# A five-stage graph network on one core: in message layers two to five the addition of edge features and the relu take an octet of row tiles by one instruction each

## The reference, cut to what matters

```
for l in range(5):
    h_in = h + vn[batch]
    emsg = relu(h_in[src] + edge_attr @ We[l] + be[l])
    agg  = segment_sum(emsg, dst, num_segments=4096)
    t = h_in + agg
    t = relu(t @ W1[l] + b1[l]) @ W2[l] + b2[l]
    ...                      # normalisation, relu but in the last layer
    h = t + h_in
```

## Time and profile before

| what | value |
| --- | --- |
| median of 3 runs | 9367.71 us (9363.5 to 9368.68) |
| profiled execution | 9374.53 us |
| its span, first to last instruction | 9372.7 us |
| mean granted TensorE clock | 0.786 of full speed |
| TensorE matmuls busy | 6152.2 us, 66% |
| VectorE busy | 3611.3 us, 39% |
| ScalarE busy | 1609.9 us, 17% |
| GpSimd busy | 5231.5 us, 56% |

### The profile page before, as it was taken

How to read it: one execution, slowest core, us unless ns; L and a number is a source line. 1 busy time by engine, 2 the same in 40 slices (tenths; PEclk the granted TensorE clock), 3 DMA queues, 4 the chain that set the end, 5 groups by cost and what they waited for, 6 DMA issues and landing times. The chain is left out here.

```text
span 9372.7 us, 114718 instructions
## 1 busy us (share of the span) xinstructions
PE 6152.2 (66%) x28483; PEld 4699.3 (50%) x28484; DVE 3611.3 (39%) x5667; ACT 1609.9 (17%) x3223; POOL 5231.5 (56%) x5128
## 2 busy tenths in 40 slices
PE   3667667765776667556856783656666666666666
PEld 2556545654565456445644562444453453454345
DVE  4445434443443334334543453545561121122123
ACT  1222212221222112212200013332330000000000
POOL 3555465546554655555557744543316676766666
PEclk8889878887888788778877886777786776777677
DMA  4333333333333333333333315554423332332333
GB/s 121 105 100 99 99 106 97 96 96 104 102 93 97 105 101 96 98 105 100 105 92 87 89 58 190 197 177 158 144 86 92 95 93 87 93 94 83 90 95 89
DMA packets 434518, 987.02 MB, mean 105 GB/s; under 512 B 124176, under 2 KB 210832, under 8 KB 417936
## 3 DMA queue, kind: packets, MB, share of 16 engines
q0 software_dynamic: 245760, 673.51, 25.1%
q1 hardware_dynamic: 128816, 194.88, 6.3%
q10 hardware_dynamic: 59744, 116.68, 3.8%
HBM read 845.23 MB, written 139.46 MB: 105 GB/s over the span
## 5 line engine op out<-in xcount | busy, mean ns | idle before, releaser
L371 POOL DMA_INDIRECT ring<-node_table,idx x4608 | 4711.4, 1022 | 3306.6 <-issue 2091.2
L382 PE MATMUL psE<-ring,shared 128*128 128x256 f32 x3072 | 1027.7, 471 | 449.0 <-issue 338.3
L987 DVE TENSOR_TENSOR ring<-ring,psE 128x1024 f32<-128x1024 f32 x640 | 762.5, 1218 | 1048.8 <-issue 436.1
L382 PEld LDWEIGHTS psE<-ring,shared 128*128 128x128 f32 x3072 | 660.7, 229 | 791.6 <-issue 502.0
L263 DVE SCALAR_TENSOR_TENSOR shared<-iota,block_start,dst_f 128x1024 f32<-128x1024 f32 x352 | 450.8, 1286 | 1395.0 <-remote 817.4
L1364 POOL DMA_INDIRECT ring<-att_table,idx x512 | 519.2, 1014 | 764.8 <-ACT idx L1568 496.1
L851 ACT ACTIVATE ring<-ring 128x1024 f32<-128x1024 f32 x640 | 661.9, 1060 | 937.2 <-DVE ring L987 673.8
L397 PE MATMUL psE<-ring,stk 128*128 128x256 f32 x1984 | 545.5, 429 | 248.8 <-DVE stk L263 133.6
L691 PE MATMUL psE<-we_stk,stk 128*128 128x256 bf16 x2560 | 394.5, 296 | 451.1 <-issue 161.8
L382 PE MATMUL psAT<-ring,shared 128*128 128x256 f32 x2560 | 653.1, 410 | 47.9 <-issue 47.9
L382 PE MATMUL psAT<-ring,S 128*128 128x256 f32 x2560 | 649.6, 409 | 30.1 <-issue 30.0
(11 more groups left out here) (356 smaller groups left out, 7018.0 us busy)
## 6 DMA issues: line engine op xcount, KB each, us to landing
ring<-node_table,idx POOLq DMA_INDIRECT x4608
rows_table<-ring SPq DMA_DIRECT2D x64, 1072.0 KB
ring<-rows_table ACTq DMA_DIRECT2D x64, 1072.0 KB
stk<-stack_table SPq DMA_DIRECT2D x128, 512.0 KB
node_table<-tab ACTq DMA_DIRECT2D x251, 128.0 KB
stack_table<-stk SPq DMA_DIRECT2D x64, 256.0 KB
ring<-att_table,idx POOLq DMA_INDIRECT x512
tab<-in_x ACTq DMA_DIRECT2D x35, 128.0 KB
```

Of the source, the lines that this page charges most:

```text
L371: nc.gpsimd.indirect_dma_start(ring[:, q, 0:gw], None, table, bass.IndirectOffsetOnAxis(ap=idx[:, RING * half + q:RING * half + q + 1], ax ...
L382: ins = nc.tensor.matmul(bank, hots[:, u, :], ring[:, U * ob + u, 0:D], start=False, stop=True, skip_group_check=True)
L987: nc.vector.tensor_tensor(ring[:, q:q + 4, 0:D], ring[:, q:q + 4, 0:D], psE[:, 4 * D * g:4 * D * g + 4 * D].rearrange("p (u f) -> p u f", ...
```

## The change

In message layers two to five (l > 0) one addition and one relu take all eight row tiles of an octet. The addition waits for eight gathers and both halves of the encode, and signals `added[0]` alone; the relu waits for that and signals `message[0]` alone. The encode of the next octet waits for `added[0]` before its first half and for nothing before its second; the first unit waits for `message[0]` at tile 0 alone. The first message layer is as before.

```diff
@@ encode, TensorE
                         for g in halves:
-                            if not first:
+                            if not first and (l == 0 or g == 0):
                                 pe.wait_ge(added[g], at_pe)
@@ ready, TensorE, before the matmuls of the first unit
-                                if u % 4 == 0:
+                                if u % (4 if l == 0 else U) == 0:
                                     pe.wait_ge(message[u // 4], at_pe)
@@ ScalarE
-                            for g in halves:
+                            for g in halves if l == 0 else (0,):
                                 q = U * ob + 4 * g
+                                tiles = 4 if l == 0 else U
                                 act.wait_ge(added[g], at_act)
-                                nc.scalar.activation(ring[:, q:q + 4, 0:D], ring[:, q:q + 4, 0:D], ACT.Relu
+                                nc.scalar.activation(ring[:, q:q + tiles, 0:D], ring[:, q:q + tiles, 0:D], ACT.Relu
                                                      ).then_inc(message[g], 1)
@@ VectorE
-                            for g in halves:
+                            for g in halves if l == 0 else (0,):
                                 q = U * ob + 4 * g
-                                for t in range(q, q + 4):
+                                tiles = 4 if l == 0 else U
+                                for t in range(q, q + tiles):
                                     dve.wait_ge(gathered[t], landed)
 
                                 dve.wait_ge(encoded[g], at_dve)
-                                nc.vector.tensor_tensor(ring[:, q:q + 4, 0:D], ring[:, q:q + 4, 0:D],
-                                                        psE[:, 4 * D * g:4 * D * g + 4 * D].rearrange(
-                                                            "p (u f) -> p u f", u=4), ALU.add).then_inc(added[g], 1)
+                                if l > 0:
+                                    dve.wait_ge(encoded[1], at_dve)
+                                nc.vector.tensor_tensor(ring[:, q:q + tiles, 0:D], ring[:, q:q + tiles, 0:D],
+                                                        psE[:, D * 4 * g:D * (4 * g + tiles)].rearrange(
+                                                            "p (u f) -> p u f", u=tiles), ALU.add).then_inc(added[g], 1)
```

## The result

The changed kernel took 9400.98 us (median of 6 runs, 9375.85 to 9418.46) against 9365.60 us for the kernel before in the same comparison (6 runs, 9346.53 to 9379.42): ratio 1.0036, interval 1.0019 to 1.0053, that is 35 us and 18 to 50 by the interval. Two later comparisons of the same pair, on two chips, gave 1.0012 (0.9998 to 1.0025) and 1.0020 (1.0006 to 1.0034). The three, weighted by their intervals, give 1.0021, some 20 us slower.

What follows compares the result with a forecast made beforehand. No engine is near full; what counts is which engine is late, and that changes within a layer. Losses of 1.2, 4.2 and 1.8 us a layer gave 29 us, 9397 on the median, plus 3: 9400; range 9352 to 9455.

Steps and rivals of the forecast that it cites:

- (a): Layer start: the next encode starts behind the whole addition, 1.07 us later, plus some 0.1 for waits; 1.2 us a layer.
- (b): Last 11 to 12 octets of a layer: first unit waits for the whole relu, 0.35 us an octet, 4.2 a layer.
- TensorE is paced by its own chain: End of a layer: hidden-layer matmuls, their relu, turn, encode, first and further unit set TensorE's pace; no size given.
- R2: End of a layer: further unit or hidden relu absorbs the first unit's delay; 0 to 18 us remain, 9377; chance 0.19.
- (c): Middle, about octets 5 to 51: delays between a gather burst's start and the silence's end are swallowed; 1.8 us a layer kept.
- (d): Stack loads, VectorE's next one-hot, GpSimd's queue: loads 1 us later cost nothing, and GpSimd gets no new instruction.
- R1: Message layers: silences move, every delay is kept, 22 us a layer, 90 in all, 9458; chance 0.12 including anything towards the forecast.
- silences: Middle of a layer: VectorE and TensorE nearly idle from late instructions, recovering about 3 us after a gather burst's last.
- Code loading: Middle of a layer: a taken branch forces a DMA instruction fetch, tying a silence to that moment; no size given.
- R3: Starved stretch: ScalarE's missing relu gives back 0.7 us a turn, 45 us less the 29: 16 us faster, 9352; chance 0.12.

Runs made afterwards that it cites:

- late_halves: Kernel before with its two additions and two relus, but everything that follows waits until both halves are done: 9372.21 us, ratio 1.0019.
- one_add: Changed kernel with its one wide addition, but the relu in two halves with two signals: 9370.07 us, ratio 1.0017.
- one_relu: Kernel before with two additions, but one wide relu behind both: 9342.22 us, ratio 0.9991; repeated, 9362.77 us, ratio 1.0002.
- before_pad: Kernel before with one more ScalarE register instruction (adding 0) per octet in layers two to five: 9360.92 us, ratio 1.0000.
- relu_twice: Changed kernel with its wide relu carried out twice in layers two to five: 9438.17 us, ratio 1.0086 to the kernel before.

## Why the prediction was right, and where it was not

The forecast was 9400, 32 us over the median, on a sum of 29; measured were 35 us in the first comparison and some 20 over the three, both within the 14 to 48 of its bounds. The sign and the size held, but the size by luck as well: 24 of the 29 us stood on terms of which the runs show 4 or 5. By terms:

**(a) The encode and gathers at the layer's start.** Predicted 1.2 us a layer; the gathers resume 1.3 us a layer later, 5.4 in four, of which 4.3 are the later signal and 1.1 the longer wait in front of the addition. Right. late_halves and one_add have it too (gathers 6.1 and 5.4 us later than before in four layers), one_relu has not, and of these only the two that have it are slower than the kernel before by more than their interval.

**(b) The first unit behind the relu.** Its first half held: 0.35 us an octet were taken and the first unit starts 1.45 instead of 1.08 us after the encode, 0.37 more. Its second half failed. "TensorE is paced by its own chain" is the step that was wrong. Paid by all of 12 octets the delay would be 4.2 us a layer; 1.0 a layer is what three profiles of each show for octets 52 to 63 (4.2 in all, one pair of them +11.5, the others +0.2 and +1.0). The octets without a hidden relu, and the last, do pay it in full, 4.9 us in four layers. In the octets from 55 to 60 TensorE waits before the turn for a hidden relu that stands at encode + 12.8 us whether the matmuls before it ended 4.65, 3.90 or 3.34 us earlier. The first unit's delay comes out of that wait of TensorE, 2.4 us in the median before and 1.6 with the change, and costs nothing; with the relu done twice the wait is used up in half of these octets, and they pay 23 us. This is rival R2's mechanism. What I held against it, "that idle time is caused by a relu that itself waits for matmuls behind the first unit, so it moves along", was read from the order of the program and not from the trace, whose lines on L712 and L805 above have the matmuls done 4.66 us before the relu. Its "remote" as the relu's releaser said as much. Why the relu stands there is open: it needs the gathers beside it (0.04 us behind the matmuls without them), and ScalarE's own DMA issue before it is a cause that no run excludes.

**(c) The middle swallows.** Right, and stronger than taken: 1.8 us a layer were predicted, -0.4 measured, which is nothing within the scatter. Without gathers the same octets pay 38 us, and octets 0 to 12 another 29; with them, nothing that shows.

**(d) Nothing elsewhere.** one_relu's two results and before_pad agree. VectorE's and ScalarE's saved busy time bought nothing.

**R1**, rigid silences, is out: the changed kernel would be 90 us slower and relu_twice some 489. Code loading, which would have tied a silence to a branch, is out as its cause: no transfer of instructions starts in the stretch of the silences. (The range of the forecast ends at "R1's 9455", where R1 was worked out as 9458; nothing hangs on it.) **R3**, gains by fewer instructions, is out as far as ScalarE's missing instruction goes: one more of them costs under 14 us in before_pad, and one_relu gained nothing when repeated. **R2** describes the end of a layer; its time, 9377 or up to 18 us over before, lies beside the joint result, and the forecast's 9400 beside the first comparison.

The three ratios say some 20 us (12 to 27 by their joint interval). Some 10 of it are located: the 5.4 of (a) and the 4.9 of the octets that pay (b). That they add up to a cost is argued, as one_relu has the second kind and is not slower. The ratios put the cost to the late `added` (late_halves +17 us, one_add +15) and not to the relu (-13 and +3), with intervals that barely part; through which octets the rest comes stays open.

## What to carry to other kernels

When an engine waits and the trace names nobody that it waits for, compare the wait's end with the end of its true producer. Where the producer was done microseconds before, the pace comes from elsewhere, and a delay in the chain is free up to the wait that it shortens: here up to TensorE's 2.4 us before the turn. Merging two instructions saves little on an engine that is idle half the time and moves every follower's start to the end of the whole; whether that costs is decided by what the follower's follower waits for. Before reading a stretch of a profile, see how far it repeats, and split it where two kinds of steps are summed. A doubled instruction is a cheap probe, and its result can have the other sign: here the largest gain of the study, 2.1%, came from an instruction that changes no value.

## What the runs showed of the hardware

- Beside GpSimd's indirect gathers some instructions come late, but not whatever waits for a signal. A message relu of ScalarE started 0.03 to 0.04 us after its addition in all 251 cases beside a burst; the hidden relu, behind ScalarE's own DMA issue, began 4.65 us after its matmuls in the median of the late octets, and 0.04 us without gathers; 341 of 5,120 register and branch instructions of VectorE took around 0.7 us instead of 45 ns, none without gathers. What holds them is open.
- Without gathers message layers two to five take some 350 us less each over 63 octets, more than a third of their time; waits for gathered rows were 46 us in all. TensorE was then busy for 493.0 of 494.3 us at a granted clock of 1.00, and with gathers for 584 of 850 at 0.82 to 0.83.
- A VectorE operation with both inputs in SBUF (128x2048 fp32, 2.295 us) stretches a gather that it overlaps, from 0.95 us to 1.83 in the mean of 407; the stretched ones end 0.82 us after it. One with an input in PSUM does not (0.96). With the stretch the pauses between bursts became fewer and the kernel 2.1% faster. Why is open.
- Three chips ran the same kernel at medians of 9302, 9355 and 9360 us.
